# Two attention layers with experts on one core: queries and keys transposed by their projection and placed by transfers

## The reference

```
h = layernorm(x) * (1 + ca) + sa
x = x + ga * attention(h)
h = layernorm(x) * (1 + cb) + sb
x = x + gb * experts(h)
```

```
output = merge(softmax(q k^T * SCALE) v) @ Wo + bo
rq = output @ Wrq + brq                    # recursive queries
rk, rv = past @ Wrk + brk, past @ Wrv + brv   # two past states of 256 tokens
rec = mean over the two pasts of softmax(rq rk^T * SCALE) rv
gate = sigmoid([output, rec] @ Wg + bg)
attention = output * (1 - gate) + rec * gate
```

## Time and profile before

| | |
|---|---|
| median of 3 runs | 938.25 us (938.09 to 940.03) |
| profiled execution, span from first to last instruction | 918.6 us |
| profiled execution's own time | not given by the profile beside its span |
| mean granted TensorE clock, share of full speed | 0.956 |
| busy in the span | TensorE 852.7 us, VectorE 733.2, ScalarE 585.7, POOL 279.3 |
| bytes moved by transfers | 48.38 MB |

### The profile page before, as it was taken

One profiled execution on the slowest core, in us unless ns is written; L12 is line 12 of the kernel. 1 busy time (PEld: TensorE's weight loads), 2 busy tenths in 40 slices (PEclk: granted clock), 3 DMA queues, 4 the chain that ended last, 5 costly groups with the idle time before them and its releaser, 6 DMA issues.

```text
span 918.6 us, 19243 instructions
## 1 busy us (share of the span) xinstructions
PE 852.7 (93%) x6883; PEld 543.4 (59%) x6883; DVE 733.2 (80%) x2133; ACT 585.7 (64%) x1277; POOL 279.3 (30%) x423
## 2 busy tenths in 40 slices
PE   7799999998788899999999999999999999888994
PEld 6456666565488875445444544445454444888993
DVE  6888888888457787997989887988999984787774
ACT  2457676666556526798879877878777876343331
POOL 7123232425511445402310020201105622335332
PEclk9899999999979998999999998999999996979997
DMA  4424320011112113800000000000071100102123
GB/s 138 108 60 139 98 65 24 13 25 30 43 30 84 53 38 115 277 2 2 2 1 2 2 1 2 1 1 1 1 256 44 49 1 16 45 26 81 49 71 108
DMA packets 47927, 48.38 MB, mean 53 GB/s; under 512 B 5606, under 2 KB 39398, under 8 KB 47576
## 3 DMA queue, kind: packets, MB, share of 16 engines
q1 hardware_dynamic: 39784, 38.03, 14.2%
q0 software_dynamic: 3296, 6.82, 2.3%
q10 hardware_dynamic: 4752, 2.30, 0.8%
HBM read 30.83 MB, written 21.02 MB: 56 GB/s over the span
## 4 chain that ended last, share of the span: by engine, by line
PE 65%; DVE 24%; issue 3%; POOL 3%; ACT 2%; DMA 2%; SPq 0%; DVEq 0%; POOLq 0%; ACTq 0%
PE pv L1781 15%; PE st L1758 9%; PE ring L1749 9%; DVE M L2082 7%; PE ring L1650 5%; PE ring L1895 5%; PE st L1650 4%; PE st L1880 3%; DVE M L2089 3%; DVE ring L2086 3%; PE ring L1661 2%; PE ring L1711 2%; PE st L1873 2%; PE st L1888 2%; PE pv L1888 1%
## 5 line engine op out<-in xcount | busy, mean ns | idle before, releaser
L1507 ACT ACTIVATE Et<-st 128x512 f32<-128x512 f32 (+3 forms) x768 | 374.0, 551 | 121.0 <-PE st L1758 117.0
L2089 DVE TENSOR_REDUCE M<-ring 128x1 f32<-128x512 f32 x256 | 160.1, 683 | 29.3 <-PE ring L1749 29.2
L2082 DVE TENSOR_REDUCE M<-ring 128x2 f32<-128x512 f32 x256 | 159.9, 681 | 13.4 <-PE ring L1749 13.0
L2086 DVE CUSTOM_DVE_ANT_0 ring<-ring,maskw 128x128 f32<-128x128 f32 (+3 forms) x256 | 121.8, 509 | 24.4 <-PE ring L1749 23.0
L1781 PE MATMUL pv<-Et,Va 128*32 128x256 f32 (+3 forms) x1536 | 136.4, 416 | 1.8 <-POOL Et L1321 1.6
L1749 PE MATMUL ring<-Kbd,Qa 128*128 128x128 f32 (+3 forms) x256 | 88.6, 368 | 9.7 <-DVE M L2086 6.7
L1321 POOL TENSOR_SCALAR_AFFINE_SELECT Et<-Et 128x256 f32<-128x256 f32 x128 | 53.2, 418 | 135.2 <-ACT Et L1507 133.4
L1758 PE MATMUL st<-Qb,Kbd 128*128 128x512 f32 (+3 forms) x256 | 84.6, 351 | 4.9 <-ACT Et L1507 4.6
L1781 PE MATMUL pv<-Et,RV 128*32 128x256 f32 x1024 | 86.4, 409 | 1.0 <-ACT PVs L1514 1.0
L1749 PE MATMUL ring<-RKT,Qa 32*128 32x512 f32 x256 | 80.7, 504 | 4.3 <-DVE M L2082 2.6
L1758 PE MATMUL st<-Qb,KT 32*128 32x512 f32 x256 | 75.6, 506 | 0.0
(11 more groups left out here) (295 smaller groups left out, 1515.4 us busy)
## 6 DMA issues: line engine op xcount, KB each, us to landing
Xd<-Xd SPq DMA_DIRECT2D x8, 1056.0 KB, 16.7
L1W<-in_L1W SPq DMA_DIRECT2D x2, 2048.0 KB, 12.4
Kbd<-Ksb SPq DMA_DIRECT2D x60, 64.0 KB, 2.0
Xs<-Xd SPq DMA_DIRECT2D x39, 66.0 KB, 1.9
W<-in_L0W SPq DMA_DIRECT2D x8, 258.0 KB, 3.9
W<-in_L0W SPq DMA_DIRECT2D x8, 256.0 KB, 4.2
G<-Zd SPq DMA_DIRECT2D x8, 256.0 KB, 4.1
Yd<-Yt ACTq DMA_DIRECT2D x30, 64.0 KB, 1.6
```

The lines of the kernel that those rows point to most:

```text
L1507: e.activation(Et[s // 2 % 4][:, j % 2, q0:512], bank(ph)[:, q0:512], ACT.Exp, scale=SCALE).then_inc(exp_done, 1)
L2082: e.tensor_reduce(M[i][:, t, j, :], bank(ph)[:, :].rearrange("p (two n) -> p two n", two=2), AX.X, ALU.max).then_inc(mx_red, 1)
L2086: e.tensor_tensor_reduce(bank(ph)[:, 0:n], bank(ph)[:, 0:n], maskw[:, 512 - n:512], 1.0, -3e38, ALU.add, ALU.max, M[i][:, t, j, 0:1]).then ...
L2089: e.tensor_reduce(M[i][:, t, j, 0:1], bank(ph)[:, 0:n], AX.X, ALU.max).then_inc(mx_red, 1)
```

## The change

Queries and keys of a batch are projected with the weights as the stationary operand, so they come out with heads on partitions and tokens along the row: phases `pq` and `pk` (one product of 512 columns each), and V apart in `vp` (four products of 128 columns, a bias product in layer 2). The biases of queries and keys are added by ScalarE in the eviction. A phase `split` cuts them into upper half and rest: VectorE masks, POOL subtracts (VectorE for the first batch). A phase `stage` on SP stores the pieces into DRAM tensors `Dq` and `Dk` with 32 rows a head, whose rows 24 to 31 were filled at the start from an input `rows8` (zeros, or -1 for the keys). Per unit `ldq` and `ldk` load 4 heads: the queries into one of four tiles `Qs` (one transfer of 256 KB), the keys into `Kbd` (four transfers) or `KT` (one).

The maxima go into small tiles `Mc`, which one TensorE transpose (`mT`) turns; ScalarE evicts 32 or 64 rows into `Ms`, and SP places them in the queries' rows with four transfers (`mput`). The score products of `st` wait for these and read the same `Qs` as `mx`. `QK`, `Qa`, `Qb` and `Ksb`, and the phases `kT`, `qT`, `qbT`, `qkv2`, `rq2` and `zQK` are gone. All weight loads, zeros and wipes move from SP's order to ScalarE's. In layer 2, from the third unit on, one product of ones stands before the score product of head 2 in each token tile, the first of that tile (FILL). The core of the diff:

```diff
+NQ = 4
-KPREP, QPREP, FRONT, BACK = (2, 5), 7, (10, 12), (34, 36)
-AFTER_MAX, FINISH, PREP = (4, 3), (2, 5), (-24, -23)
+KPREP, QPREP, FRONT, BACK = (3, 4), 0, (10, 12), (34, 36)
+AFTER_MAX, FINISH = (2, 3), (2, 5)
-ST_TAKES = ("kT", "qT", "qbT")
+ST_TAKES = ("mT",)
-WARM = (8, 6, 3, 18)
+WARM = (8, 6, 3, 24)
+FILL = 1
 def ones_ahead(ph):
-    return 2 if ph[0] == "mx" and ph[1] == 1 and ph[2] < 2 and ph[4] % 2 == 0 else PAD.get(ph, 0)
+    if ph[0] != "mx" or ph[1] == 0:
+        return 0
+    if ph[2] < 2:
+        return 2 if ph[4] % 2 == 0 else 0
+    return FILL if ph[4] == 2 else 0
...
-        for t in range(4):
-            do("qkv", l, b, k, t)
+        for what in ("pq", "pk", "vp", "split"):
+            do(what, l, b, k)
             yield
-        do("qkv2", l, b, k)
+        do("stage", l, b, k)
...
         yield from wait(AFTER_MAX[l])
-        do("qbT", l, u)
+        do("mT", l, u)
         flags.add(("shifted", l, u))
+        yield
+        do("mput", l, u)
...
# SP
+                elif what == "stage":
+                    sp.wait_ge(q_high, n + 1)
+                    for piece in (0, 2):
+                        e.dma_start(Dq[slot][:, 8 * piece:8 * piece + 8, :], hq[:, :]).then_inc(q_staged, 16)
+                    sp.wait_ge(q_low, n + 1)
+                    e.dma_start(Dq[slot][:, 8:16, :], Xq[:, :]).then_inc(q_staged, 16)
...
+                elif what == "ldq":
+                    sp.wait_ge(*q_stored(l, k))
+                    if n >= NQ:
+                        sp.wait_ge(st_full, n_st["st", l_, u_, 3, 3] + 1)
+                    e.dma_start(Qs[n % NQ][:, :].bitcast(F32), Dq[k % 2][4 * g:4 * g + 4, :, :].rearrange("j r n -> (j r) n")
+                                ).then_inc(q_in[n % NQ], 16)
+                elif what == "ldk":
+                    if l == 0:
+                        for j in range(4):
+                            e.dma_start(Kbd[u % 3][32 * j:32 * j + 32, j, :].bitcast(F32), Dk[slot][4 * g + j, :, :]
+                                        ).then_inc(kbd_in[u % 3], 16)
+                    else:
+                        e.dma_start(KT[u % 3][:, :].bitcast(F32), Dk[slot][4 * g:4 * g + 4, :, :].rearrange("j r n -> (j r) n")
+                                    ).then_inc(kt_in[u % 3], 16)
+                elif what == "mput":
+                    wide = 4 if units[l][u][0] == "rec" else 2
+                    sp.wait_ge(*taken(("mT", l, u)))
                     for j in range(4):
+                        e.dma_start(q[32 * j + 24:32 * j + 24 + wide, :].bitcast(F32),
+                                    Ms[l][u % 2][4 * wide * j:4 * wide * j + 4 * wide, :]).then_inc(m_in[u % 2], 16)
...
# POOL
+                elif what == "split" and n_split[ph]:
+                    pool.wait_ge(q_high, n_split[ph] + 1)
+                    e.tensor_tensor(Xq[:, :], Xq[:, :], hq[:, :], ALU.subtract).then_inc(q_low, 1)
...
# ScalarE
+                elif what == "mT":
+                    if u >= 2:
+                        act.wait_ge(*m_ready(l, u - 2))
+                    act.wait_ge(misc_full, filled(ph))
+                    e.activation(Ms[l][u % 2][0:rows, :], bank(ph)[0:rows, 0:128], ACT.Copy).then_inc(act_took, 1)
...
# TensorE
+                elif what in ("pq", "pk"):
+                    nc.tensor.matmul(bank(ph)[:, :], wqkv[l][:, n0:n0 + 128], hT[:, :], start=True, stop=True).then_inc(misc_full, 1)
...
+                elif what == "mT":
+                    pe.wait_ge(mcol_done, n_mcol["mcol", l, u] + 1)
+                    nc.tensor.transpose(bank(ph)[:, 0:128], Mc[l][u % 2][:, :], ident[:, :]).then_inc(misc_full, 1)
...
                 elif what == "st":
-                    pe.wait_ge(*taken(("qbT", l, u)))
+                    pe.wait_ge(*m_ready(l, u))
```

More of the change, by code:

```diff
@@ L190, in clearing @@
     def clearing():
-        for what in ("QK1", "Va1", "Kbd2"):
+        for what in ("Va1", "Kbd2"):
             do("clear", what)
@@ L490, in prep_next @@
         yield
-        for t in range(4):
-            do("qkv", 1, 0, 0, t)
+        for what in ("pq", "pk", "vp", "split"):
+            do(what, 1, 0, 0)
             yield
-        do("qkv2", 1, 0, 0)
+        do("stage", 1, 0, 0)
         yield
-        yield
-        do("qT", 1, 0)
-        do("kT", 1, 0)
+        do("ldq", 1, 0)
+        do("ldk", 1, 0)
     def past_prep():
@@ L611, in plan @@
     do("brow", 1)
-    for t in range(4):
-        do("qkv", 0, 0, 0, t)
+    for what in ("pq", "pk", "vp", "split"):
+        do(what, 0, 0, 0)
     do("warm", 3)
-    do("qkv2", 0, 0, 0)
+    do("stage", 0, 0, 0)
     do("brow", 2)
     do("brow", 3)
-    do("qT", 0, 0)
-    do("kT", 0, 0)
+    do("ldq", 0, 0)
+    do("ldk", 0, 0)
     at = STEPS0
@@ L760, in program @@
         qa0 = top[0]
-        Qa = [sb(f"Qa{i}", [128, 512], F32R) for i in range(2)]
-        Qb = [sb(f"Qb{i}", [128, 512], F32R) for i in range(2)]
+        Qs = [sb(f"Qs{i}", [128, 512], F32R) for i in range(NQ)]
         Et = [sb(f"Et{i}", [128, 2, 512]) for i in range(4)]
@@ L766, in program @@
         ksb0 = top[0]
-        Ksb = [sb(f"Ksb{i}", [128, 512], F32R) for i in range(2)]
+        top[0] += 4096
         xh0 = top[0]
@@ L1090, in _ @@
                     load("cols2", cols2[:, :], d["cols2"])
-                    sp.wait_ge(ld["wqkv0"], 16)
-                    load("mask", maskw[:, :], d["mask"])
-                    load("wm0r", wmod[0][:, 256:768], d["wmod0"][:, 256:768])
-                    for b in range(1, NB):
-                        load(f"x{b}", x[:, 4 * b:4 * b + 4, :], d["x"][b].rearrange("(t p) n -> p t n", p=128))
-                    load("wo0", wo[0][:, :], d["wo0"])
-                    load("wm1", wmod[1][:, :], d["wmod1"])
@@ L1237, in _ @@
                     e.memset(onesM[:, :], 1.0).then_inc(z_ones, 1)
[L1238 removed]
                     clear_va(0)
+                    for i in range(2):
+                        ins = e.memset(Mc[0][i][:, :], 0.0)
+                    ins.then_inc(z_mc, 1)
                     e.memset(brow[:, :].bitcast(F32), 0.0).then_inc(z_brow, 1)
@@ L1322, in _ @@
                                     channel_multiplier=-1).then_inc(cut_done, 1)
-                elif what == "zQK":
-                    pool.wait_ge(y_full, before(ph, "output"))
-                    pool.wait_ge(comb_done, before(("between",), "combine"))
-                    for i in range(4):
-                        pool.wait_ge(y_stored[0][i], 16 * len(range(i, len(TILES[0]), 4)))
-                    pool.wait_ge(mx_full, before(ph, "mx"))
-                    clear_qk(1).then_inc(z_qk, 1)
                 elif what == "clearRV":
@@ L1414, in experts_over, with load @@
                     act.wait_ge(y_stored[0][i], 16 * len(range(i, len(TILES[0]), 4)))
+            def load(key, out, src):
+                e.dma_start(out, src).then_inc(ld[key], 16)
             def evict(ph, out, func=ACT.Copy, **kw):
@@ L1947, in halves @@
                 return e.tensor_tensor(lo, src, hi, ALU.subtract)
-            def qk_free(ph, l, k):
-                p = qk_let_go(ph, l, k)
-                if p is not None:
-                    dve.wait_ge(misc_full, filled(p))
-                dve.wait_ge(z_qk, 3 if l == 1 and k % 2 else k % 2 + 1)
             def gated(out, src, gate):
@@ L2169, in _ @@
                         hT_free(ph)
+                        for l_ in range(2):
+                            dve.wait_ge(zeroed[l_], 16 * sum(part[0] == l_ for part in ZERO_PARTS))
                     settle()
```

491 lines of the change are left out of this document (236 added, 255 removed).

## The result

The changed kernel takes 1045.76 us in the median (1039.95 to 1051.56), the one before 938.2: a ratio of 1.114, interval 1.1095 to 1.1185. Forecast were 922 us, 888 to 948. It is slower, far outside the range. Single executions of a kernel can lie some per cent above its fastest; ratios here leave out those more than 1.5% above it.

What follows compares the result with a forecast made beforehand. TensorE was taken to bound layer 1 and heavy units of layer 2, VectorE light units. Start +3, layer 1 -13, between +2, layer 2 -8 gave -16 us: 922 us, range 888 to 948.

Steps and rivals of the forecast that it cites:

- The new path behind the maxima: Transposed maxima to first score product: 3.6 us against covers of 3.3 and 3.5; charged +4 in layer 2, +6 in layer 1.
- B: Rival, chance 0.16: the maxima's four transfers land late at each unit's first score product; +20 us (958), +35 at full.
- The ones: Layer 2, before the first maximum of each tile: 120 products on TensorE at 0.232 us, 27.8 us.
- Hidden: 0: Storing and reloading queries and keys costs 0 us, hidden behind other steps; loads moved to ScalarE 0, at most 5.
- The start: Before the first maximum: splitting, storing and reloading the first queries and keys adds 2 to 4 us, taken as +3.
- Between the layers: Layer 2's first maxima wait for keys cut, stored and reloaded, ready at 332 to 335 us: +2 us.
- TensorE's relief: Turns of queries and keys go: TensorE net -21 us in layer 1, -15.5 in layer 2; counted -14 and -12.
- A: Rival, chance 0.27: small transfers hide whole, TensorE's relief counts in full; -46 us together, 892 us.
- the prediction's rule: Layer 2's attention: three quarters of TensorE's net saving count as time, its slack being small.
- C: Rival, chance 0.07: without turns TensorE's clock falls to 0.90 for 0.97 in layer 2; +19 us, 941 us.
- D: Rival, chance 0.05: the turns were off the path, as the ones are, and nothing moves; 938 us.
- the marks set beforehand: Wrong if: first score product waits over 1.3 us for DMA, light units exceed 11.8, or first maxima wait for query loads.

Runs made afterwards that it cites:

- a: Changed kernel without the products of ones (FILL = 0): 1030.94 us, ratio 1.093 to the kernel before.
- d_noput_fill0: Changed kernel without the transfers of the maxima and without the products of ones: 964.15 us, ratio 1.018 to the kernel before.
- k: Changed kernel without ones, loads on SP, split stores by GpSimd, past blocks' load by ScalarE, experts' weights in 24 pieces: 995.82 us, ratio 1.085.
- m_free: Changed kernel with loads, stores and weights rearranged, without ones and without the transfers of the maxima: 951.22 us, ratio 1.010 to the kernel before.
- b_fill1: Kernel before with the 120 products of ones added in layer 2, nothing else: 979.92 us, ratio 1.040.
- n_free_turns: m_free with eight transposes of the identity added for each unit of layer 2: 958.84 us, ratio 1.019 to the kernel before.
- c_noput: Changed kernel without the transfers of the maxima, products of ones kept: 1006.40 us, ratio 1.066 to the kernel before.
- l_combo0_mput2: The kernel of k, with two of the four transfers of the maxima issued by ScalarE: 976.53 us, ratio 1.063 to the kernel before.

## Why the prediction was wrong

**The new path behind the maxima** is the first step that failed. It was priced at 3.6 us (3.3 to 5.3) against a cover of 3.3. The light unit above has 5.4: an issue into the queries' rows is 0.62 to 0.65 us, where I took 0.4, nearer to stores, and passed over the 0.59 of the key blocks, the only issues of the earlier trace rows between on-chip tiles; ScalarE adds 0.7; and in units with a batch's stores SP is 1.6 us late, though the prediction listed the stores. TensorE's stalls, 18.2 us for the 10 charged, were not far off. What neither the forecast nor B had is the second price: behind a stall of 2 us the clock is at its lower level, for 4 to 50 us, and a light unit there takes 19.2 us for 13. Leaving the transfers out gives 4.8 points with the ones, 7.5 without them (a against d, and k against m).

**The ones**, 0.232 us each by the warming run. There they follow their like; between 32-row products one takes 0.42 and parts a pair that runs in the time of one. 27.8 us, of which three quarters were charged, became 36 in the kernel before.

**"Hidden: 0"** for placing queries and keys and for ScalarE's loads. The start was forecast at +3 and is +10 in the trace: ScalarE issues loads until 13.1 us and evicts only then, the last key store is issued at 19.04 for 14.9 and has landed at 25.6, 6 us after its issue for 2.5 to 4. Between the layers, forecast +2, it is +6, some 3 of them the chip's by b_fill1: a store of 4.3 and a reload of 2.9 us stand behind the last expert's products. The past blocks' load was not seen: behind `stage` in SP's order it costs 8.8 us of TensorE. Nor were the experts' weights, harmless before, since in layer 2 nothing on the path came by a transfer.

**TensorE's relief**, -14 and -12 us (A: -21 and -25), is hardly there even where nothing stands against it. In d_noput_fill0, with ones and transfers gone, layer 1 is 1.6 us shorter and its light unit 9.4 us as before; light units of layer 2 fall from 11.3 to 10.8, to VectorE's 9.9 and the writes. Without the ones the prediction's rule gives -33 us for layer 2's 31 units, -23 for the 22 from the fourth to the 25th; there it is -7.9 (277.8 for 285.7). I read the turns' share of the chain as time that goes with them; most of it went to the next wait. This alone would have undone the forecast's -16; m_free, where the start and the way between the layers are longer too, ends at 1.010.

**The rivals.** A's premise is tested by m_free, and false. B named the late transfers and, with +20 to +35 us, a fifth to a third of the loss. C named the clock, and layer 2 is at 0.84 for 0.97. The missing turns are the smaller part of that: n_free_turns puts some back and gains clock, not time, while without the stalls c_noput is at 0.97 in 400 to 700 us. D was right on the turns, not on the ones. Of the marks set beforehand, first score products did wait over 1.3 us (2.6) and light units were over 11.8 (13.0); first maxima waited for loads of keys (10.7 and 3.9 us), not of queries.

Open: why FRONT 10 lowers the clock as it does; why the lower clock lasted 50 us behind one stall and 4 behind two others; what the `remote` waits are; and how much of the remaining 6.3 points of l_combo0_mput2 a shorter way for the maxima would give back. No version here beats the kernel before.

## What to carry to other kernels

A result that the next step needs within a few microseconds should not come by a transfer whose queue also carries stores and weights: count the way from the last writer to the first reader with every issue at the duration of its own kind, and list what else that queue holds. Where TensorE runs at full clock with little slack, price a stall not by its length alone but also by the work that runs at the lower clock behind it. And before work is added or removed beside a bound engine, time it in its place: a product of ones cost twice its row, and transposes with 8% of layer 1's chain were worth 1% of it.

## What the runs showed of the hardware

- Two pairs of 32-row products side by side took 0.43 us, the time of one pair; a full 128 x 128 product of 128 columns between them 0.42, 0.32 between a group of turns and a 32-row pair, 0.232 in a row of its like.
- Behind three stalls of 1.9 to 2.1 us and one of 1.31 (789.03) TensorE ran at the lower clock, once for 50 us and three times for 4 to 6, busy throughout; behind stalls of 0.42 and 0.51 us (558.05, 544.75) it stayed at full clock.
- A transfer of 4 or 8 KB between on-chip tiles took SP 0.62 us to issue, one of 1 or 2 KB to a scratch tensor in HBM 0.25, and one such 9.5 behind 6.3 MB of weights on the same queue. Size and target differ together, so which of them makes the difference is not shown.
- The kernel before took 917.5 to 918.5 us on three chips, at granted clocks of 0.95 to 0.965, and 944 and 944.5 on two others, at 0.924 to 0.952. All profiles from the latter two have `remote` waits of ScalarE and VectorE, those from the three none.
